# Attention in a four-stage kernel: the maxima lead by 10 tiles in place of 12, and half of the row transfers are issued by ScalarE

## The chip, the cores and the metric

The kernel runs on one core of one Trainium2 chip. The metric is the device time of one execution in microseconds (us): the median of several executions. A core has five engines that run their own instruction streams and meet only at semaphores: TensorE (PE; PEld is its weight load), VectorE (DVE), ScalarE (ACT), GpSimd (POOL) and the sync engine (SP), which computes nothing and issues transfers. An instruction that issues a transfer (a DMA) stands in the stream of the engine that issues it; the transfer itself runs on 16 DMA engines.

## The reference

The reference is a transformer of four stages on `x` of 4 x 1024 x 256: attention, a ternary feed-forward layer, a state-space layer, and a mixture of 16 experts. The change is in the attention alone:

```python
q = (x @ Wq).reshape(Bx, Tx, H, d).transpose(0, 2, 1, 3)     # H = 16 heads, d = 16
k = ...; v = ...
attn = (jnp.einsum('bhqc,bhkc->bhqk', q1, k_eff1) + jnp.einsum('bhqc,bhkc->bhqk', q2, k_eff2)) * scale
attn = jax.nn.softmax(attn, axis=-1)
out = jnp.einsum('bhqk,bhkd->bhqd', attn, v)
```

## The kernel before

The attention works in 16 **units**, each of four heads of one batch. A unit is computed twice over.

The **first pass** (`first_pass`, L2184) computes scores with queries on the partitions, in 32 **tiles** per unit, each of one head and 128 queries against all 1024 keys: two matmuls of 512 columns. VectorE reduces each tile to the negated maximum of every row (L2035). Two tiles fit in PSUM (`PAIRS = 2`), so a tile waits for the reduction of the tile two before it. A group of 16 tiles (`AHEAD`) covers half a unit, that is one half of the queries (`qc`) of four heads. When a group is complete, GpSimd splits the maxima into a high and a low part (`negated_rows`, L2100), VectorE turns them by a transpose (`turn_rows`, L2042, two tiles after the group's last, `TURN = 2`), and the rows are copied by DMA (L2137) from `nmT` to rows 48 and 49 of each half of the query buffer `KQ`: eight transfers (`ROWS`), each 2 x 8 x 32 elements, four for each half `y` of the partitions.

The **second pass** (L2238) computes the scores transposed, in 64 **blocks** per unit, each 128 keys against 512 queries of one head. The copied rows are part of its operand, so that the maximum is subtracted inside the matmul. ScalarE takes the exponential of a block (L2073) into `PR`, and TensorE weighs the values with it (L2220, in two parts for each step of four blocks). Three blocks fit in PSUM (`SLOTS = 3`): block `s` waits for the exponential of block `s - 3`. Twice per half unit ScalarE copies a half of the sums out (`keep_heads`, L2060), behind the exponentials of blocks 0 and 2.

One loop on TensorE weaves the two: block `s`, then one matmul of the tile that lies `AHEAD + LEAD` tiles on, then in every second block a part of the weighing. So two blocks go with one tile, and `LEAD` says how many tiles a group's maxima are done before the group's own scores begin. Ahead of the loop TensorE computes tiles 2 to `AHEAD + LEAD - 1` alone; at the end of the loop, where no tile is left, it repeats tiles of the last unit (`again`), so the loop is equally long for any `LEAD`. The order on each engine is the order in which the code is written.

The sync engine does, for each unit: eight transfers of heads done (`heads`, L2148 and L2149), nine loads of a later unit (L229), the rows of `(u, 1)`, nine loads, the rows of `(u + 1, 0)`. The group's first block waits for all eight rows:

```python
if kt == 0 and h == 0:
    pe.wait_ge(row_loaded[u % RING], 16 * ROWS * (QC * (u // RING) + qc + 1))
if BLOCKS * u + s >= SLOTS:
    pe.wait_ge(exp_done, BLOCKS * u + s - SLOTS + 1)
```

Of the kernel before, what the change touches and what calls it, by code (L numbers as in the profile page):

```python
# [6 lines left out]
F32 = mybir.dt.float32  # L7
# [9 lines left out]
P = 128  # L17
# [14 lines left out]
UNITS = BATCH * H // HG  # L32
# [3 lines left out]
QC = SEQ // BANK  # L36
PARTS = 2
PAIR_Q = [0, 1, 0]
PAIR_K = [0, 0, 1]
KROWS = len(PAIR_Q) * HD  # L40
AROWS = KROWS + PARTS
HALF = P // 2
HR = HG // 2
RING = 3
# [95 lines left out]
def transformer_kernel(nc, ins, out):  # L140
# [27 lines left out]
    with outer:  # L168
# [10 lines left out]
        with mid:  # L179
            ffw = FeedForwardWeights(sbuf, mid)  # L180
            with ExitStack() as st:
# [80 lines left out]
                with ExitStack() as s2:  # L262
# [6 lines left out]
                    def banks_free(eng, n):  # L269
                        if n < 3 * DK:  # L270
                            eng.wait_ge(lo_ready, 2 * DK * NC + n)
                        else:
                            eng.wait_ge(v_kept, NC + 1)
                    att = attention(nc, sem, s2, sbuf, ps, KQ, queries, kq_loaded, load_qk, V, slot, sums, maxima, packed, heads_moved, weighed,
                                    invert_sums, spread_inverses, weigh_heads, ffw, ident, projected, parts_stored, banks_free)
                    def opening_sync(sp):
# [1714 lines left out]
def attention(nc, sem, stack, sbuf, ps, KQ, queries, kq_loaded, load_qk, V, slot, sums, maxima, packed, heads_moved, weighed, invert_sums, spread_inverses, weigh_heads, ffw, ident, projected, parts_stored, banks_free):  # L1991
# [10 lines left out]
    mx, nmp, nmT = maxima.mx, maxima.nmp, maxima.nmT  # L2002
# [3 lines left out]
    vo_set, ones_ready = sem("vo_set"), sem("ones_ready")  # L2006
    row_loaded = [sem(f"row_loaded{r}") for r in range(RING)]
    st_done, exp_done, pv_done = sem("st_done"), sem("exp_done"), sem("pv_done")
    max_done, red_done = sem("max_done"), sem("red_done")
    nm_hi, nm_lo, nm_turned = sem("nm_hi"), sem("nm_lo"), sem("nm_turned")  # L2010
# [6 lines left out]
    LOADS = (2 + 2 * QC) * len(PAIR_Q)  # L2017
    QH = QT // QC
    AHEAD = HG * QH
    LEAD = 12  # L2020
    TURN = 2
    WPARTS = 2
    PART = BANK // WPARTS
# [2 lines left out]
    st_bank = lambda u, s: ST_BANK + (BLOCKS * u + s) % SLOTS  # L2026
    half = lambda h, n: slice(HALF * (h // HR), HALF * (h // HR) + n)
    of_tile = lambda kq, h, q: kq[half(h, KROWS), q // QH, h % HR, q % QH * P:(q % QH + 1) * P]

    def vector(dve):  # L2030
        def reduce(u, t):
            h, q = order[t]
            b = max_bank(u, t)
            dve.wait_ge(max_done, MAXES * u + t + 1)
            nc.vector.tensor_reduce(mx[:, u % RING, h * QT + q:h * QT + q + 1], ps[:, b:b + 2].rearrange("p a n -> p (a n)"), AX, ALU.max, negate=True).then_inc(red_done, 1)  # L2035

        def turn_rows(u, qc):

            dve.wait_ge(nm_lo, QC * u + qc + 1)
            if u > 0:  # L2040
                dve.wait_ge(row_loaded[(u - 1) % RING], 16 * ROWS * (QC * ((u - 1) // RING) + qc + 1))
            nc.vector.transpose(nmT[:, qc], nmp[:, qc].rearrange("p y a m -> p (y a m)")).then_inc(nm_turned, 1)  # L2042

        for u in range(UNITS):
            for t in range(MAXES):
                reduce(u, t)
                if u % 2 == 1 and u > 1 and t == 2 * LEAD:
                    invert_sums(dve, u // 2 - 1)
                groups, past = divmod(MAXES * u + t + 1, AHEAD)
                if groups > 0 and past == TURN:  # L2050
                    turn_rows((groups - 1) // QC, (groups - 1) % QC)
        turn_rows(UNITS - 1, QC - 1)

    def scalar(act):
        def keep_heads(u, qc, part):

            act.wait_ge(pv_done, WPARTS * (STEPS * u + KT * (qc + 1) - 1) + part + 1)
            if u > 0:
                act.wait_ge(heads_moved, 16 * MOVES * u)
            nc.scalar.copy(OT[:, qc * BANK + part * PART:qc * BANK + (part + 1) * PART],  # L2060
                           ps[:, OT_BANK, part * PART:(part + 1) * PART]).then_inc(ot_kept, 1)

        ffw.magnitudes(nc, act, kept)
        for h in range(2):
            parts_stored(act, h)
        for u in range(UNITS):
            for s in range(BLOCKS):
                step, h = s // HG, s % HG
                kt = step % KT
                act.wait_ge(st_done, BLOCKS * u + s + 1)  # L2070
                if h == 0 and STEPS * u + step >= 2:
                    act.wait_ge(pv_done, WPARTS * (STEPS * u + step - 1))
                nc.scalar.activation(PR[:, kt % 2, h], ps[:, st_bank(u, s)], ACT.Exp).then_inc(exp_done, 1)  # L2073
                if kt == 0 and h % 2 == 0:
                    if step > 0:
                        keep_heads(u, 0, h // 2)
                    elif u > 0:
                        keep_heads(u - 1, 1, h // 2)
        for part in range(WPARTS):
            keep_heads(UNITS - 1, 1, part)  # L2080
# [46 lines left out]
                pool.wait_ge(weighed, PIECES * ((u - 1) // 2))  # L2127

    def sync(sp):
        def rows(u, qc):  # L2130
            sp.wait_ge(nm_turned, QC * u + qc + 1)
            for g in range(P // 32):
                for y in range(2):
                    row, of = HALF * y + KROWS, 32 * g + 16 * y
                    src = nmT[of:of + PARTS * HR * QH, qc]
                    dst = queries(u % RING)[row:row + PARTS, qc].rearrange("a h (q n) -> a (h q) n", n=P)[:, :, 32 * g:32 * (g + 1)]
                    sp.dma_start(dst.bitcast(F32), src).then_inc(row_loaded[u % RING], 16)  # L2137

        def heads(u):


            sp.wait_ge(ot_kept, WPARTS * QC * (u + 1))
            b, g = u // UPB, u % UPB
            pair = u // 2
            for h in range(HG):
                to = HALF * (g % 2) + HD * h
                one = 2 * HD * h + HD
                sp.dma_start(slot(b)[to:to + HD, g // 2], OT[2 * HD * h:2 * HD * h + HD, :]).then_inc(heads_moved, 16)  # L2148
                sp.dma_start(packed[to:to + HD, pair % 2], OT[one:one + 1, :].rearrange("a (r n) -> a r n", r=HD)).then_inc(heads_moved, 16)  # L2149

        projected(sp)
        ffw.load(sp)
        for h in range(2):
            parts_stored(sp, h)
        rows(0, 0)
        for u in range(UNITS):
            if u == 0:
                sp.wait_ge(ones_ready, 2)
            if u > 0:
                heads(u - 1)  # L2160
            for some in (range(LOADS // 2), range(LOADS // 2, LOADS)):
                if u + 2 < UNITS:
                    sp.wait_ge(st_done, BLOCKS * u)
                    load_qk(sp, u + 2, (u + 2) % RING, some)
                if some.start == 0:
                    rows(u, 1)
            if u + 1 < UNITS:
                rows(u + 1, 0)
            if u == 2:
                sp.wait_ge(ffw.steps, ffw.quantised)  # L2170
            if u > 0 and u % 2 == 0:
                spread_inverses(sp, u // 2 - 1)
        heads(UNITS - 1)
# [21 lines left out]
    def tensor(pe):  # L2195
# [27 lines left out]

        for t in range(PAIRS, AHEAD + LEAD):
            for k in range(QC):
# [3 lines left out]
        for u in range(UNITS):  # L2229
            kq = KQ[u % RING]  # L2230
            for s in range(BLOCKS):
# [8 lines left out]
                t, k = divmod(s, QC)  # L2240
                ahead = MAXES * u + AHEAD + t + LEAD
                if ahead < MAXES * UNITS:
# [9 lines left out]
    def heads_kept(pe):  # L2252
        pe.wait_ge(ot_kept, WPARTS * QC * UNITS)

    return AttentionPrograms(vector, scalar, gpsimd, sync, tensor, first_maximum, heads_kept)


# [24 lines left out]
```

## Time and profile before

| | us |
|---|---|
| runs | 1662.2, 1668.51, 1669.74 |
| median | 1668.51 |
| the profiled execution's own time | 1661.44 |
| its span (first to last instruction) | 1659.7 |
| the attention's loop, first to last exponential | 126.2 to about 778 |
| mean granted clock of TensorE | 0.931 |

The trace gives for each instruction its start and duration. A line number is that of the kernel before; ACTq and SPq are instructions that the engine's sequencer carries out itself, such as the issue of a transfer or a wait for a semaphore.

### The profile page before, as it was taken

To read this page: it belongs to the slowest core of one execution; us is meant where nothing else is said; L and a number is where in the kernel's file an instruction comes from. 1 tells how busy PE (TensorE), PEld (TensorE's weight loads), DVE (VectorE), ACT (ScalarE), POOL (GpSimd) and SP (SyncE) were. 2 spreads that over 40 slices of the span, in tenths; PEclk is the share of its full clock that TensorE was granted. 3 is DMA by queue.
4 is the path that set the end of the run, shared out by engine and by line. 5 is a ranking of instruction groups with operands and counts; after the bars stand their busy time and mean duration, and the time that the engine had idled before them with its cause. 6 is when DMAs were issued, how large, how long until landed. Compare 5 with 4: busy or idle time off the path is not lost. (4 is left out here: it accounts for less than half of the span.)

```text
span 1659.7 us, 39722 instructions
## 1 busy us (share of the span) xinstructions
PE 1495.5 (90%) x14095; PEld 986.6 (59%) x14097; DVE 1160.0 (70%) x2105; ACT 988.0 (60%) x2035; POOL 428.2 (26%) x703
## 2 busy tenths in 40 slices
PE   6999999999999999999999968899695499999990
PEld 5843333333333333334788867888584399999980
DVE  7687999999999999980888857454486622222225
ACT  3426888888888888886355613344232355555543
POOL 3144501010101010100112234333330155555540
PEclk9967999999999999999999976899896599999995
DMA  6951223232322323210200002343457222222218
GB/s 222 280 173 26 47 47 61 47 60 48 60 52 55 61 49 62 48 23 9 27 1 0 1 15 53 105 105 96 124 193 234 89 70 70 70 70 70 73 57 306
DMA packets 117063, 135.27 MB, mean 81 GB/s; under 512 B 29540, under 2 KB 85880, under 8 KB 116792
## 3 DMA queue, kind: packets, MB, share of 16 engines
q1 hardware_dynamic: 104152, 107.60, 25.3%
q0 software_dynamic: 7584, 20.72, 3.9%
q10 hardware_dynamic: 5184, 4.98, 0.9%
q8 instruction: 96, 1.57, 0.4%
q14 instruction: 47, 0.39, 0.1%
HBM read 92.23 MB, written 36.04 MB: 77 GB/s over the span
## 5 line engine op out<-in xcount | busy, mean ns | idle before, releaser
L2035 DVE TENSOR_REDUCE mx<-ps 128x1 f32<-128x1024 f32 x512 | 622.8, 1221 | 26.5 <-PE ps L2184 21.2
L2073 ACT ACTIVATE PR<-ps 128x512 f32<-128x512 f32 x1024 | 557.1, 599 | 89.1 <-PE ps L2238 34.1
L2184 PE MATMUL ps<-KQ 48*128 48x512 f32 x1024 | 390.5, 463 | 3.4 <-DVE mx L2035 3.0
L2238 PE MATMUL ps<-KQ 50*128 50x512 f32 x1024 | 380.4, 451 | 0.2 <-DMA KQ<-nmT 0.2
L2220 PE MATMUL ps<-PR,VO 128*32 128x256 f32 x4096 | 331.1, 395 | 9.2 <-ACT PR L2073 8.7
L2238 PEld LDWEIGHTS ps<-KQ 50*128 50x128 f32 x1024 | 155.5, 187 | 218.0 <-ACT PR L2073 200.4
L2220 PEld LDWEIGHTS ps<-PR,VO 128*32 128x32 f32 x4096 | 80.9, 108 | 196.6 <-ACT PR L2073 98.7
L2184 PEld LDWEIGHTS ps<-KQ 48*128 48x128 f32 x1024 | 159.4, 192 | 21.2 <-DVE mx L2035 20.5
L1927 PEld LDWEIGHTS ps<-e_xinT,e_w 128*128 128x128 f32 x1264 | 155.0, 193 | 5.7 <-issue 1.7
L1927 PE MATMUL ps<-e_xinT,e_w 128*128 128x128 f32 x1264 | 155.7, 277 | 1.1 <-ACT e_xinT L1841 1.1
L1917 PE MATMUL ps<-eW,e_hiddenT 128*128 x632 | 149.4, 380 | 0.6 <-DVE e_hiddenT L1893 0.6
L2100 POOL CAST nmp<-mx 128x16 fp32r<-128x16 f32 x32 | 6.3, 196 | 530.2 <-DVE mx L2035 406.3
L1893 DVE TENSOR_SCALAR e_hiddenT<-ps,b1T 128x128 f32<-128x128 f32 x158 | 48.1, 346 | 105.4 <-PE ps L1927 99.3
L1917 PEld LDWEIGHTS ps<-eW,e_hiddenT 128*128 128x128 f32 x632 | 114.0, 190 | 13.1 <-issue 0.8
L1886 DVE TENSOR_TENSOR e_y<-ps,b2b 128x256 f32<-128x256 f32 x79 | 33.6, 425 | 115.0 <-PE ps L1917 114.7
L1823 POOL DMA_INDIRECT expert_outputs<-e_y,y_row x79 | 78.0, 987 | 123.6 <-DVE e_y L1886 123.2
L1333 PE MATMUL ps<-W 64*64 64x72 f32 (+7 forms) x1024 | 87.2, 259 | 12.0 <-DVE W L1143 8.3
L1818 POOL DMA_INDIRECT e_xin<-expert_inputs,token x79 | 76.9, 973 | 79.5 <-POOLq L1814 53.5
L1849 ACT COPY e_w<-eW 128x1024 f32 x79 | 82.6, 1046 | 22.4 <-issue 16.4
L1335 PE MATMUL ps<-W 64*64 64x64 f32 (+7 forms) x1152 | 90.9, 252 | 2.5 <-issue 2.5
L1841 ACT COPY e_xinT<-ps 128x256 f32<-128x256 f32 x79 | 29.4, 372 | 85.0 <-PE ps L1908 85.0
L1335 PEld LDWEIGHTS ps<-W 64*64 64x64 f32 x1152 | 70.9, 154 | 7.0 <-issue 7.0
(290 smaller groups left out, 2103.6 us busy)
## 6 DMA issues: line engine op xcount, KB each, us to landing
qk_parts<-parts SPq DMA_DIRECT2D x8, 2048.0 KB, 8.5
TB<-toeplitz_lines SPq DMA_DIRECT2D x32, 512.0 KB, 6.3
KQ<-qk_parts SPq DMA_DIRECT2D x96, 128.0 KB, 4.6
KQ<-qk_parts SPq DMA_DIRECT2D x192, 64.0 KB, 2.4
eW<-in_L_ffn_W SPq DMA_DIRECT2D x16, 512.0 KB, 10.5
eW<-in_L_ffn_W SPq DMA_DIRECT2D x8, 1024.0 KB, 11.9
e_got<-expert_outputs SPq DMA_DIRECT2D x16, 512.0 KB, 8.2
X<-in_L_attn_x SPq DMA_DIRECT2D x8, 512.0 KB, 4.3
```

What stands on the lines that cost most here:

```text
L1333: nc.tensor.matmul(pair(0, h)[r, s % HS, 0:c + BLK], W2[r, s, P:P + BLK], W1[r, s, P - c:P + BLK], start=True, stop=True, skip_group_check ...
L1335: last = nc.tensor.matmul(pair(1, h)[r, s % HS, 0:c + BLK], W1[r, s, P:P + BLK], W2[r, s, P - c:P + BLK], start=True, stop=True, skip_grou ...
L1818: nc.gpsimd.indirect_dma_start(xin[:, r], None, xrows, bass.IndirectOffsetOnAxis(ap=token[:, k:k + 1].bitcast(U32), axis=0)).then_inc(x_lo ...
L1823: nc.gpsimd.indirect_dma_start(y_rows, bass.IndirectOffsetOnAxis(ap=y_row[:, k:k + 1].bitcast(U32), axis=0), y[:, z], None).then_inc(store ...
L1849: nc.scalar.copy(w1[:, z].rearrange("p k h -> p (k h)"), W1[:, ds(e, 1)].rearrange("p a k h -> p (a k h)")).then_inc(w1_kept, 1)
L1917: last = nc.tensor.matmul(ps[:, Y_BANK[z], 0:D], hT[:, z, j], W2[:, ds(e, 1), j, :].rearrange("p a d -> p (a d)"), start=(j == 0), stop=(j ...
L1927: last = nc.tensor.matmul(ps[:, bank, j % HK * P:(j % HK + 1) * P], w1[:, z, dk, j * P:(j + 1) * P], xT[:, z, dk], start=(dk == 0), stop=( ...
L2035: nc.vector.tensor_reduce(mx[:, u % RING, h * QT + q:h * QT + q + 1], ps[:, b:b + 2].rearrange("p a n -> p (a n)"), AX, ALU.max, negate=Tr ...
L2073: nc.scalar.activation(PR[:, kt % 2, h], ps[:, st_bank(u, s)], ACT.Exp).then_inc(exp_done, 1)
L2184: made = nc.tensor.matmul(ps[:, max_bank(u, t) + k], of_tile(queries(u % RING), h, q), kq[half(h, KROWS), 0, h % HR, k * BANK:(k + 1) * BA ...
L2220: last = nc.tensor.matmul(ps[2 * HD * h:2 * HD * (h + 1), OT_BANK, cols], VO[:, u % 2, kt, h], PR[:, kt % 2, h, cols], start=(kt == 0 and ...
L2238: nc.tensor.matmul(ps[:, st_bank(u, s)], kq[half(h, AROWS), 0, h % HR, kt * P:(kt + 1) * P], queries(u % RING)[half(h, AROWS), qc, h % HR] ...
```

## The change

`LEAD` falls from 12 to 10. The function `rows` moves out of `sync`, takes the engine and the half `y`, and issues four transfers per call. The sync engine calls it for `y = 0` at the places where it issued all eight; ScalarE calls it for `y = 1`, once ahead of its loop and then ahead of the exponential of block 20 (rows of `(u, 1)`) and of block 52 (rows of `(u + 1, 0)`) of each unit.

```diff
-    LEAD = 12
+    LEAD = 10
...
+    def rows(eng, u, qc, y):
+        eng.wait_ge(nm_turned, QC * u + qc + 1)
+        for g in range(P // 32):
+            row, of = HALF * y + KROWS, 32 * g + 16 * y
+            src = nmT[of:of + PARTS * HR * QH, qc]
+            dst = queries(u % RING)[row:row + PARTS, qc].rearrange("a h (q n) -> a (h q) n", n=P)[:, :, 32 * g:32 * (g + 1)]
+            eng.dma_start(dst.bitcast(F32), src).then_inc(row_loaded[u % RING], 16)
...
+        act.wait_ge(ones_ready, 2)
+        rows(act, 0, 0, 1)
         for u in range(UNITS):
             for s in range(BLOCKS):
                 step, h = s // HG, s % HG
+                for qc in range(QC):
+                    if s == QC * (AHEAD * (2 - qc) + TURN - LEAD) + 4 and u + 1 - qc < UNITS:
+                        rows(act, u + 1 - qc, qc, 1)
                 kt = step % KT
                 act.wait_ge(st_done, BLOCKS * u + s + 1)
...
-        rows(0, 0)
+        rows(sp, 0, 0, 0)
...
                 if some.start == 0:
-                    rows(u, 1)
+                    rows(sp, u, 1, 0)
             if u + 1 < UNITS:
-                rows(u + 1, 0)
+                rows(sp, u + 1, 0, 0)
```

ScalarE's stream in the middle of a half unit, before. A row is a line of the code with its operation, the tile that it writes and what it waits for; `x3` is three in a row:

```order
L2073 ACTIVATE PR<-ps 128x512 [waits pv_done,st_done]
L2073 ACTIVATE PR<-ps 128x512 [waits st_done] x3
L2073 ACTIVATE PR<-ps 128x512 [waits pv_done,st_done]
L2073 ACTIVATE PR<-ps 128x512 [waits st_done] x3
L2073 ACTIVATE PR<-ps 128x512 [waits pv_done,st_done]
```

The same place after the change; L2086 is the exponential's new line number and L2036 the issue of a row:

```order
L2086 ACTIVATE PR<-ps 128x512 [waits pv_done,st_done]
L2086 ACTIVATE PR<-ps 128x512 [waits st_done] x3
L2036 DMA KQ<-nmT 2x8x32 [waits nm_turned]
L2036 DMA KQ<-nmT 2x8x32 x3
L2086 ACTIVATE PR<-ps 128x512 [waits pv_done,st_done]
```

Four issues have come between the exponential of block 19 (or 51) and that of block 20 (or 52): 31 times in the loop, and once ahead of it.

TensorE's stream where the loop begins, before (L447 is a projection of the stage in front; the first row with L2238 is the first block of the loop):

```order
L2184 MATMUL ps<-KQ 128x512 x2
L447 MATMUL ps<-wfT,xT 128x256 x12
L2184 MATMUL ps<-KQ 128x512 x52
L2238 MATMUL ps<-KQ 128x512
L2184 MATMUL ps<-KQ 128x512
```

And after:

```order
L2188 MATMUL ps<-KQ 128x512 x2
L447 MATMUL ps<-wfT,xT 128x256 x12
L2188 MATMUL ps<-KQ 128x512 x48
L2242 MATMUL ps<-KQ 128x512
L2188 MATMUL ps<-KQ 128x512
```

The stretch of first-pass matmuls ahead of the loop is four matmuls, two tiles, shorter.

## Rows read from the trace of the kernel before

**Rows 1.** The page's costliest groups: DVE's reductions (busy us, mean ns).

```profile
L2035 DVE TENSOR_REDUCE mx<-ps 128x1 f32<-128x1024 f32 x512 | 622.8, 1221 | 26.5 <-PE ps L2184 21.2
```

**Rows 2.** Two windows: busy us (instructions) of PE, PEld, DVE, ACT, POOL; clock.

```profile
720.00:740.00 20.00, 19.73 (x194) 7.33 (x192) 19.52 (x19) 17.71 (x35) 0.42 (x2) 1.00 0.08 19
740.00:760.00 20.00, 19.73 (x194) 7.24 (x194) 3.28 (x4) 17.71 (x35) 3.75 (x10) 1.00 0.14 27
```

**Rows 3.** Timeline, PE in the loop (start us, us): two blocks and the next.

```profile
301.43 0.49 PE L2238 MATMUL ps<-KQ 50*128 50x512 f32 x1
...
301.76 0.39 PE L2238 MATMUL ps<-KQ 50*128 50x512 f32 x1
...
302.09 0.64 PE L2220 MATMUL ps<-PR,VO 128*32 128x256 f32 x8
302.66 0.49 PE L2238 MATMUL ps<-KQ 50*128 50x512 f32 x1
```

**Rows 4.** Timeline, ACT and DVE from the start of a half unit.

```profile
296.21 0.37 ACT L2060 COPY OT<-ps 128x256 f32<-128x256 f32 x1 [0.24 <-PE ps L2220]
296.48 1.09 ACT L2073 ACTIVATE PR<-ps 128x512 f32<-128x512 f32 x2
...
297.71 1.61 ACT L2073 ACTIVATE PR<-ps 128x512 f32<-128x512 f32 x3
299.50 12.89 ACT L2073 ACTIVATE PR<-ps 128x512 f32<-128x512 f32 x21 [0.18 <-PE ps L2238]
303.37 0.20 DVE L2042 STREAM_TRANSPOSE nmT<-nmp 128x32 f32<-128x32 f32 x1
```

**Rows 5.** Timeline, narrow windows of ACT: exponentials of two blocks, then the next.

```profile
301.96 1.08 ACT L2073 ACTIVATE PR<-ps 128x512 f32<-128x512 f32 x2
303.19 0.60 ACT L2073 ACTIVATE PR<-ps 128x512 f32<-128x512 f32 x1
```

**Rows 6.** The row transfers' issues on SP: all, and one run of eight.

```profile
L2137 SPq DMA_DIRECT2D KQ<-nmT x256: 596/611/839, 114.4 to 750.5; - x128
187.10 5.29 SPq L2137 DMA_DIRECT2D KQ<-nmT  x8
```

**Rows 7.** Issues by ACT in the last stage (ns min/median/max), two with neighbours.

```profile
L1963 ACTq DMA_DIRECT2D out<-X x8: 378/422/1342, 1632.9 to 1654.6; - x8
1632.86 0.32 SPq L1957 DMA_DIRECT2D e_got<-expert_outputs  x1
1632.87 0.43 ACTq L1963 DMA_DIRECT2D out<-X  x1
1650.11 1.71 ACT L1970 ACTIVATE e_second<-e_got,weight 128x256 f32<-128x256 f32 x4 [1.69 <-DMA e_got<-expert_outputs]
1651.37 0.38 ACTq L1963 DMA_DIRECT2D out<-X  x1
```

**Rows 8.** A wait of ScalarE for `heads_moved` (L2059), and the exponentials beside it.

```profile
L2059 ACTq EVENT_SEMAPHORE  x1: 17/17/17, 296.6 to 296.6; - x1
L2073 ACT ACTIVATE PR<-ps x2: 603/604/605, 296.5 to 297.0; 128x512 f32<-128x512 f32 x2
```

**Rows 9.** Timeline, the end of the stretch ahead of the loop.

```profile
114.29 12.62 DVE L2035 TENSOR_REDUCE mx<-ps 128x1 f32<-128x1024 f32 x10
125.45 0.62 PE L2238 MATMUL ps<-KQ 50*128 50x512 f32 x1
```

**Rows 10.** Windows by clock: two in the loop, two in later stages; columns as rows 2.

```profile
130.00:140.00 10.00, 10.00 (x56) 3.30 (x52) 5.69 (x6) 4.52 (x9) 6.36 (x9) 0.50 0.01 3
150.00:155.00 5.00, 5.00 (x52) 1.82 (x48) 4.98 (x5) 4.33 (x8) 0.00 (x0) 1.00 0.00 0
824.00:832.00 8.00, 5.70 (x18) 4.36 (x19) 7.56 (x14) 4.77 (x8) 0.00 (x0) 0.79 0.00 0
964.00:968.00 4.00, 3.04 (x25) 3.04 (x26) 0.91 (x1) 0.00 (x0) 2.82 (x4) 1.00 0.00 0
```

**Rows 11.** Who waited for the row transfers (us, times).

```profile
  PEld ps L2238: 2.3, 5
```

More of the change, by code:

```diff
@@ L2129, in sync @@
     def sync(sp):
[L2130 to L2137, printed above, removed]
         def heads(u):
```

## The prediction

> **What bounds the kernel now.** I read first which engine paces the attention's loop, then where a wait that the change moves would land. In the windows of the loop TensorE is busy 19.73 of 20 us at full clock, VectorE 19.52 and ScalarE 17.71 [rows 2]. VectorE looks like a second bound: a reduction takes 1.221 us [rows 1], and two blocks pass each 1.23 us (PE's block matmul starts at 301.43 and 302.66) [rows 3]. The second window of rows 2 tells them apart: in it VectorE has next to nothing to do, 3.28 us, and TensorE still does 194 matmuls in 20 us, as before. So TensorE paces the loop by itself, and time that it loses there comes back nowhere: afterwards it can go no faster than 1.23 us per two blocks.
>
> ScalarE has 11% of slack on the mean, but what counts is how late one exponential may be. Take as zero the start of a block pair on TensorE. Its second block starts at +0.33 and lasts 0.39, so it is done at +0.72 [rows 3]. The two exponentials start at +0.53 (301.96) and at +1.02 (a pair of 1.08 us whose second lasts about 0.59, so it starts at 302.45); the next pair's first starts at +1.76 (303.19) and ends 0.60 later [rows 3, 5].
>
> **The two tiles less ahead of the loop.** There VectorE paces: ten reductions in 12.62 us, 1.26 us a tile [rows 9]. Two fewer take 2.5 us off the start of the loop (125.45). The early part of the loop runs at the low clock, 1.2 GHz: 56 matmuls in 10 us against 97 at full clock, and full clock is there by 150 us [rows 2, 10]. If the rise comes 2.5 us earlier too, all of 2.5 us is won; if it stays where it is, work is won at the rate 56/97, 1.4 us. I take 2.0.
>
> **The sync engine's half.** Its issues stand 5.29 us for eight, (5.29 - 0.61)/7 = 0.67 us from one to the next [rows 6]; four less at each place free 2.7 us on its queue. That buys only what now waits for the rows: 2.3 us over the whole kernel at the weight load [rows 11], of which most is hidden behind matmuls under way. I take 0.5, between 0 and 2.3. The lead that is two tiles (2.5 us) shorter costs nothing on this side, since the issues end 2.7 us earlier. In the sync engine's queue the loads behind the rows move earlier too, and nothing waits for them.
>
> **ScalarE's half, which decides.** When does ScalarE's first issue start? The rows are turned, before, at 303.57; blocks 6 to 26 of that half unit start from 299.50 and each takes (12.89 - 0.60)/20 = 0.615 us, so that is (303.57 - 299.50)/0.615 = 6.6 blocks on, within block 12 [rows 4]. (The three groups of exponentials in front are blocks 0, 1 to 2 and 3 to 5.) With `LEAD` at 10 it is four blocks later, within block 16: ahead of the issues, which stand behind the exponential of block 19. So `nm_turned` is no wait. How far may the sequencer run ahead of the engine? It passes instructions still being executed: one transfer was issued at 1651.37 while a run of four activations lasted from 1650.11 to 1651.82 [rows 7]. But it does not pass one whose own wait is open: the wait for `heads_moved` stands behind the exponential of block 2, asks for something long done, and is carried out at 296.6, when block 2's scores have just come and its exponential (297.0) still stands behind that of block 1 [rows 8]. So the first issue comes when block 19's scores are done, at +0.8 of the pair 18 and 19.
>
> How long are four issues? ScalarE issues none of this shape in the trace. The nearest rows: the same transfers from the sync engine, 0.61 us (0.596 to 0.839) [rows 6], and ScalarE's own of another shape, 0.378 to 0.43, once 1.342 [rows 7]. I take the same transfer's: the shape decides more than the engine, as the first runs of both engines are alike (0.32 to 0.43 in rows 7). Four take 3 x 0.67 + 0.61 = 2.62 us, to +3.42. The exponential of block 20 starts about 0.1 later, +3.52, in place of +1.76: 1.76 late. It ends at +4.12. Block 23 waits for it (three slots); its turn would be at 2 x 1.23 + 0.33 = +2.79. With 0.05 for the semaphore it starts at +4.17, and **TensorE stands still for 1.4 us**. Behind it the tile's second matmul and so VectorE's reduction wait too, as does the weighing. ScalarE then does its exponentials 0.49 apart and is level again before the next wait.
>
> The issues stand at 31 places in the loop. At block 20 of unit 0 the clock is low and two blocks, which are 12 matmuls, take 10 / 56 x 12 = 2.1 us [rows 10]: block 23's turn is at +4.9, and the exponential, even a us later than above, is not missed; 30 places are left: 30 x 1.4 = 42 us. Bounds: at 0.42 us an issue (0.38 and a gap) four end at +2.5, and block 23 is 0.4 to 0.5 late, some 13 us in all; at 0.84 and a gap each, +4.3, 2.3 us late, 69 us. A bound at nothing is the second rival.
>
> Do the two queues disturb each other? At 1632.86 both issued within 10 ns, and ScalarE's took 0.43, against 0.378 alone [rows 7]: 0.05 an issue, 0.2 a place, 6 us in all, within the bounds. The Trainium skill (Perfetto Trace Analysis, DMA Instruction, HWDGE) has the sequencers share one descriptor generator under a lock, and would make each of two issues at once wait for the other. The trace agrees in sign, but with a tenth of such a wait.
>
> **The sum.** 42 - 2.0 - 0.5 = +39.5 us on the profiled execution's 1661.44: 1701. The median of the runs shown lies 7.1 above that execution, so the changed kernel's median should lie between 1701 and 1708; I say **1705**. A measurement of this kernel tells about 0.5%, 8 us, from no change.
>
> **Rivals.** *The issues are hidden* (0.16). If ScalarE's sequencer ran on past open waits, the issues would begin when the rows are turned, 0.6 into block 16, which is at -0.33; they would end at +2.3, block 20's exponential would start at +2.4 and end at +3.0, and TensorE would stand for 0.25 us: 7.5 us in all, 1661.4 + 7.5 - 2.5 = 1666, or 1670 for the median, no change. For it speaks that the issues were given four blocks to spare; against it the wait of rows 8. The Trainium skill (TensorE: Matmul & The Clock Gate, Architectural detail) gives ScalarE a queue of 8 instructions, which would hold the exponentials up to block 19 with ease and gives this rival's time if issues may pass what waits in it; rows 7 show a queue, rows 8 that what follows does not pass an open wait.
>
> *The clock falls too* (0.08). In a later stage the clock fell where TensorE stood idle for 2.3 us: mean 0.79 over 8 us, so 3.4 us at 1.2 GHz; where it stood for 0.96 us it kept 2.4 GHz [rows 10]. A stop of 1.4 us lies between. If each of 30 stops cost 3.4 us at the low clock, 3.4 x (1 - 56/97) = 1.4 us more each, it is +82: 1743 to 1750.
>
> *Faster* (0.06). This needs the issues at no cost, at most 0.35 us each: four would end at +0.8 + 1.4 = +2.2 and block 20's exponential, at +2.3 to +2.9, would just not hold block 23. Then 2.5 us ahead of the loop and up to 2.3 of waits are won; and if the clock rose as soon as the loop begins, 22 us at the low rate would shrink by 22 x (1 - 56/97) = 9 us. Together 5 to 14 us, 1648 to 1656. From 0.35 an issue on it decides; every row is above that but one of the sync engine (0.32).
>
> **How the numbers follow.** The forecast has 0.70, with 1680 to 1735 as its own range (bounds 13 and 69). The range over all goes down to the hidden case and leaves out the faster one and most of the clock's: 1668 to 1735. Slower by over 0.5% (over 1677): 0.70 less a little for its lower end, and 0.08, 0.75. Within 0.5%: 0.20. Faster: 0.05.
>
> **What would show it.** Right: in the profile after, ScalarE's four issues stand about 0.65 us apart, the first about 0.8 us after the block pair starts; behind them comes the exponential 1.8 us late, and TensorE's idle time before L2242 or before its weight load grows by about 1.4 us at each of 30 places, released by ScalarE; the loop's windows show about 93% of the matmuls per us; the loop starts 2.5 us earlier. Wrong: issues of under 0.4 us, or issues that begin before block 19's scores are done, or a granted clock under 1.00 between 150 and 780 us.

## The result, and the profile after

The changed kernel takes 1773.61 us in the median of four runs (1755.11 to 1812.54), against 1668.92 us before: a ratio of 1.056 (interval 1.051 to 1.060). That ratio is over the two lower runs of the changed kernel alone, 1755.11 and 1761.71; the other two, 1785.51 and 1812.54, had a lower mean clock still (0.882 and 0.868, against 0.897 and 0.901), and the ratios below leave out such executions likewise, while each median counts all. The profiled execution took 1761.71 us, span 1760.0 us, 100.3 us longer than before. The forecast was 1705, in 1668 to 1735: the sign was right and the size far too small.

The place that the prediction worked out, in the timeline (start, duration, engine, what). TensorE's rows L2242 are blocks 18 to 23; ACTq L2036 are ScalarE's issues:

```profile
279.79 0.49 PE L2242 MATMUL ps<-KQ 50*128 50x512 f32 x1
...
280.12 0.39 PE L2242 MATMUL ps<-KQ 50*128 50x512 f32 x1
...
280.56 0.62 ACTq L2036 DMA_DIRECT2D KQ<-nmT  x1
280.81 0.59 ACT L2086 ACTIVATE PR<-ps 128x512 f32<-128x512 f32 x1
281.02 0.49 PE L2242 MATMUL ps<-KQ 50*128 50x512 f32 x1
...
281.22 1.92 ACTq L2036 DMA_DIRECT2D KQ<-nmT  x3
281.35 0.39 PE L2242 MATMUL ps<-KQ 50*128 50x512 f32 x1
...
282.25 0.50 PE L2242 MATMUL ps<-KQ 50*128 50x512 f32 x1
...
283.24 2.77 ACT L2086 ACTIVATE PR<-ps 128x512 f32<-128x512 f32 x5 [1.84 <-PE ps L2242]
283.89 0.49 PE L2242 MATMUL ps<-KQ 50*128 50x512 f32 x1 [1.14 <-ACT PR L2086]
```

With 279.79 as zero: the first issue comes at +0.77 (forecast +0.8), while block 19's exponential has not begun; the fourth ends at 283.14, +3.35 (+3.42); block 20's exponential starts at +3.45 (+3.52), and block 23, due at 282.58, starts at 283.89, 1.31 us late (1.4). These rows show the chain step by step. The last row names ScalarE as the releaser, and PE's idle time as 1.14 us, because block 22's matmul is still counted as busy.

Over the loop, the same view of waits as [rows 11] was taken from, 160 to 850 us (engine, line, who for, us in total, times, longest):

```profile
PE ps L2242 <- ACT PR L2086: 31.2, 26, 1.4
```

And the windows of the loop, columns as in [rows 2], with one ahead of them and one stop close up:

```profile
95.00:150.00 55.00, 50.30 (x244) 20.66 (x244) 49.22 (x44) 25.55 (x57) 29.97 (x51) 0.69 0.37 91
...
200.00:300.00 100.00, 95.66 (x780) 33.70 (x778) 79.86 (x71) 71.79 (x139) 15.21 (x51) 0.83 0.23 44
300.00:400.00 100.00, 95.44 (x750) 33.54 (x746) 76.68 (x68) 69.03 (x133) 7.46 (x30) 0.80 0.25 45
400.00:500.00 100.00, 94.24 (x830) 33.99 (x830) 85.71 (x76) 75.60 (x145) 8.29 (x34) 0.91 0.25 45
500.00:600.00 100.00, 93.10 (x834) 33.69 (x838) 84.97 (x74) 77.50 (x149) 7.86 (x32) 0.93 0.25 44
600.00:700.00 100.00, 95.67 (x780) 33.81 (x777) 79.90 (x71) 71.75 (x139) 7.91 (x32) 0.83 0.24 45
700.00:800.00 100.00, 92.95 (x890) 34.33 (x886) 91.44 (x81) 81.50 (x158) 9.69 (x42) 1.00 0.25 48
800.00:850.00 50.00, 47.45 (x384) 16.76 (x384) 33.74 (x30) 35.44 (x69) 4.16 (x12) 0.83 0.09 19
...
204.00:207.00 3.00, 1.80 (x18) 0.69 (x20) 1.52 (x3) 1.30 (x3) 2.46 (x10) 1.00 0.03 4
207.00:215.00 8.00, 8.00 (x52) 2.62 (x48) 4.82 (x4) 4.46 (x9) 1.00 (x3) 0.53 0.01 2
215.00:236.00 21.00, 21.00 (x120) 6.88 (x120) 12.37 (x11) 10.96 (x22) 1.83 (x10) 0.50 0.41 61
...
306.00:348.00 42.00, 42.00 (x242) 13.81 (x240) 24.61 (x21) 22.11 (x42) 1.83 (x10) 0.51 0.26 45
...
500.00:507.00 7.00, 6.12 (x46) 2.00 (x46) 4.05 (x4) 4.88 (x10) 0.00 (x0) 0.76 0.01 2
```

The window from 700 to 800 is what had been forecast: clock 1.00 and 890 matmuls in 100 us, 93% of the 956 before (4778 in 500 us over the same loop). All the other windows from 200 us on hold fewer per us, and a lower clock. The clock fell right behind a stop: TensorE does 1.80 us of work between 204 and 207, then runs at 0.53, and stays at 0.50 through 21 us in which it is never idle. Of the 650 us between 200 and 850, (0.17 + 0.20 + 0.09 + 0.07 + 0.17) x 2 x 100 + 0.17 x 2 x 50 = 157 us went at 1.2 GHz; before, none of the loop's 500 us from 200 to 700 did.

Not every stop did this. In windows of 1 us the clock is low in eight stretches between 160 and 850 us, and each begins within 2 us behind the end of a stop; the other 18 of the 26 stops left it at 1.00. The eight stretches differ much: 3.4 us at 1.2 GHz for the shortest (the window from 500 to 507), 41 us for the longest (306 to 348), 157 in all. The stops themselves are alike, 1.13 to 1.40 us of idle time.

These parts nearly add up to the change. Stops: the 26 of the line above and one more at 850.44, at about 1.4 us, 38. Low clock: at 56 matmuls per 10 us in place of 97 [rows 2, 10], 157 x (1 - 56/97) = 66 us. Against them the front: by 150 us TensorE had done 244 matmuls since 95 us, against 188 before, worth 56 / 9.7 = 5.8 us, because the loop began 2.2 us earlier (123.26) and the clock rose earlier. 38 + 66 - 6 = 98 us, of the 100.3 measured.

### The profile page after: what moved, and what is told of

Its sections match the earlier page's. It is cut to its first block and busy times, and to the rows that moved or that the text cites. A ratio compares the mean times of both kernels' runs of the same rounds, so it can differ in the third digit from the quotient of the medians.

```text
span 1760.0 us, 39715 instructions
## 1 busy us (share of the span) xinstructions
PE 1559.4 (89%) x14091; PEld 1003.3 (57%) x14093; DVE 1162.6 (66%) x2105; ACT 985.5 (56%) x2035; POOL 428.3 (24%) x703
## 5 line engine op out<-in xcount | busy, mean ns | idle before, releaser
L2086 ACT ACTIVATE PR<-ps 128x512 f32<-128x512 f32 x1024 | 554.1, 600 | 182.3 <-PE ps L2242 143.9
L2242 PE MATMUL ps<-KQ 50*128 50x512 f32 x1024 | 420.2, 488 | 33.6 <-ACT PR L2086 33.5
L2188 PE MATMUL ps<-KQ 48*128 48x512 f32 x1024 | 428.2, 499 | 3.8 <-DVE mx L2043 3.8
L2224 PE MATMUL ps<-PR,VO 128*32 128x256 f32 x4096 | 360.9, 427 | 7.7 <-ACT PR L2086 7.3
L2242 PEld LDWEIGHTS ps<-KQ 50*128 50x128 f32 x1024 | 170.7, 203 | 286.2 <-ACT PR L2086 253.1
L2188 PEld LDWEIGHTS ps<-KQ 48*128 48x128 f32 x1024 | 174.1, 208 | 19.7 <-DVE mx L2043 19.0
L1333 PEld LDWEIGHTS ps<-W 64*64 64x64 f32 x1024 | 65.6, 149 | 24.6 <-DVE W L1143 12.9
```

What stands on the lines that cost most here:

```text
L1333: nc.tensor.matmul(pair(0, h)[r, s % HS, 0:c + BLK], W2[r, s, P:P + BLK], W1[r, s, P - c:P + BLK], start=True, stop=True, skip_group_check ...
L2188: made = nc.tensor.matmul(ps[:, max_bank(u, t) + k], of_tile(queries(u % RING), h, q), kq[half(h, KROWS), 0, h % HR, k * BANK:(k + 1) * BA ...
L2224: last = nc.tensor.matmul(ps[2 * HD * h:2 * HD * (h + 1), OT_BANK, cols], VO[:, u % 2, kt, h], PR[:, kt % 2, h, cols], start=(kt == 0 and ...
L2242: nc.tensor.matmul(ps[:, st_bank(u, s)], kq[half(h, AROWS), 0, h % HR, kt * P:(kt + 1) * P], queries(u % RING)[half(h, AROWS), qc, h % HR] ...
```

## The experiments

Theory: ScalarE's four issues in a row outlast the slack of the next exponential, TensorE stops for 1.3 to 1.4 us, and the stop costs the clock. Rivals: the shorter lead makes the rows late; each issue costs its time wherever it stands; the clock falls for another reason. The ratios are to the kernel before on the same chip, which had medians of 1663.27 (the first four experiments), 1667.67 (two issues at a time, three and one, the first copies, LEAD 8) and 1665.37 us (the longer copies, LEAD 9).

**The lead alone.** Edit to the kernel before:

```diff
-    LEAD = 12
+    LEAD = 10
```

> The kernel before with LEAD 10 and nothing else: all eight row transfers stay with the sync engine. Theory (ScalarE's issues stop TensorE, and the stops cost the clock): no stop, clock 1.00 from about 150 us to the end of the loop, 1663 to 1671 us, that is the time of before less up to 2.5 us. Rival (the shorter lead makes the rows late): TensorE waits for KQ<-nmT at many group starts, and most of the 105 us of the change are here too, 1700 us or more.

1659.34 us, ratio 0.998 (0.994 to 1.001); that is below the range expected, but on this chip the kernel before, too, took 1663.27 us and not 1668.92. The loop is at full clock as before, and the waits for the rows at the weight load are 2.2 us, for 2.3:

```profile
200.00:700.00 500.00, 493.30 (x4775) 182.70 (x4772) 487.20 (x430) 442.98 (x846) 53.44 (x211) 1.00 0.29 54
```

The lead loses nothing. A gain of 0.15% (2.5 us) would lie inside this interval; it is not shown.

**ScalarE's half alone.** Edit to the changed kernel:

```diff
-    LEAD = 10
+    LEAD = 12
```

> The changed kernel with LEAD back at 12: ScalarE still issues four rows at a time, at blocks 16 and 48. Theory: the same stops of 1.3 to 1.4 us at 30 places and the same falls of the clock, 1745 to 1810 us. Rival (the shorter lead makes the rows late): 1669 us, or 1710 if only the stops are left.

1789.07 us, ratio 1.070 (1.063 to 1.078), mean clock 0.85 from 200 to 700 us. So the loss comes with the issues by ScalarE and not with the lead. It is no smaller than the change's: in its trace 14 of 28 stops were followed by a low clock, 188 us in all from 160 to 890, where the changed kernel has 8 and 157.

**One issue at a time.** The four issues stand ahead of blocks 20, 22, 24 and 26 (and 52 to 58):

```diff
-                    if s == QC * (AHEAD * (2 - qc) + TURN - LEAD) + 4 and u + 1 - qc < UNITS:
-                        rows(act, u + 1 - qc, qc, 1)
+                    n, rest = divmod(s - (QC * (AHEAD * (2 - qc) + TURN - LEAD) + 4), 2)
+                    if rest == 0 and 0 <= n < 4 and u + 1 - qc < UNITS:
+                        rows(act, u + 1 - qc, qc, 1, range(1 * n, min(1 * (n + 1), 4)))
```

The last argument of `rows` is new: it says which of the four transfers a call issues.

> The changed kernel, but ScalarE's four issues of a half unit stand apart, one ahead of the exponentials of blocks 20, 22, 24 and 26 (52, 54, 56, 58). Theory (what costs is that four issues in a row outlast the slack of one exponential): one issue of 0.62 us ends 1.4 us after the pair's start, before the next exponential's turn at 1.76, so no stop, clock 1.00 in the loop, 1662 to 1671 us. Rival (each issue costs its 0.62 us wherever it stands, 124 x 0.62 = 77 us, or the second queue disturbs the transfers): 1710 us or more.

1665.04 us, ratio 1.000 (0.997 to 1.003), clock 1.00 from 200 to 700 us with 4764 matmuls, against 4778. The same 124 issues, on the same engine, cost nothing that shows when each fits the slack. The rival that prices each issue at 0.62 us falls.

**The stop filled.** Five more matmuls behind the tile's matmul in blocks 22 and 54:

```diff
-                if ahead < MAXES * UNITS:
-                    first_pass(pe, ahead // MAXES, ahead % MAXES, k)
-                else:
-                    again(ahead, k)
+                for _ in range(1 + (5 if s in (22, 54) else 0)):
+                    if ahead < MAXES * UNITS:
+                        first_pass(pe, ahead // MAXES, ahead % MAXES, k)
+                    else:
+                        again(ahead, k)
```

> The changed kernel with five more matmuls after the tile's matmul in blocks 22 and 54, each a repeat of that same matmul into the same bank, so nothing else is computed: TensorE has work of 5 x 0.21 = 1.1 us in the stop of 1.3 us that follows. Theory (about 40 us are the stops themselves and the rest the clock that falls because TensorE stands idle in them): the stops' time stays, the clock stays at 1.00, 1700 to 1715 us. Rival (the clock falls for another reason, or the rest of the loss is something else): low clock as in the changed kernel, 1745 us or more.

1709.80 us, ratio 1.023 (1.018 to 1.027). The medians are further apart, 46.5 us or 2.8%. ScalarE's side is as in the changed kernel, the same issues and the same gap, but TensorE now works through it: the sixfold row is the tile's matmul with its five repeats, and block 23 starts 1.64 us behind block 22, as at 283.89 above:

```profile
277.06 0.62 ACTq L2036 DMA_DIRECT2D KQ<-nmT  x1
...
277.72 1.92 ACTq L2036 DMA_DIRECT2D KQ<-nmT  x3
279.74 7.70 ACT L2086 ACTIVATE PR<-ps 128x512 f32<-128x512 f32 x13 [1.83 <-PE ps L2242]
...
278.75 0.50 PE L2242 MATMUL ps<-KQ 50*128 50x512 f32 x1
278.75 1.66 PE L2188 MATMUL ps<-KQ 48*128 48x512 f32 x6
280.39 0.50 PE L2242 MATMUL ps<-KQ 50*128 50x512 f32 x1
```

Its loop in one window shows the clock at 1.00:

```profile
200.00:700.00 500.00, 492.42 (x4559) 191.45 (x4557) 456.73 (x401) 410.37 (x790) 50.01 (x196) 1.00 0.27 50
```

A half unit is 16 pairs of blocks of 12 matmuls in the trace, 192, and now 192 + 5. So 4559 of them are 23.1 half units of 21.6 us, against 500 / (4778 / 192) = 20.1 us before: 1.5 us a half unit. The delay by ScalarE is all there, and only TensorE's idleness is gone. The profiled executions are 1761.71 - 1709.83 = 52 us apart. Against the 66 us worked out above stand two more stops here (30 places, as the one in unit 0 fell into low clock, where the changed kernel's trace has 28), 3 us, and a slower start of this trace, 179 matmuls from 95 to 150 us for 244, 6.7 us: 66 - 3 - 6.7 = 56.

**How long a stop may be.** Two issues ahead of blocks 20 and 24 (52 and 56), then three and one, with the edit of the one-at-a-time experiment at two and at three a place, four blocks apart:

> The changed kernel, with ScalarE's four issues in two pairs, ahead of the exponentials of blocks 20 and 24 (52 and 56). Theory (the issues cost only what outlasts the slack): two issues end 0.77 + 0.65 + 0.62 = 2.04 us after the pair's start, the exponential runs from 2.14 to 2.74, and block 23's turn is at 2.80: a stop of under 0.1 us, 1663 to 1671 us, clock 1.00 in the loop. Rival (the cost goes by the number of issues): half of the changed kernel's stops at twice the places, 1700 us or more.

> The changed kernel, with three of ScalarE's issues ahead of block 20 (52) and the fourth ahead of block 24 (56). Theory: three issues end at 2.69, the exponential ends at 3.40, block 23 stands 0.65 us, at 30 places 20 us: 1683 to 1692 us if a stop of that length leaves the clock at 1.00. If it costs the clock too: 1700 us or more, with stretches of 0.50 in the loop. I expect the first.

1666.48 us, ratio 1.001 (0.998 to 1.003), for two at a time; 1681.89 us, ratio 1.009 (1.006 to 1.012), for three and one. The loop's window of two at a time, then that of three and one:

```profile
200.00:700.00 500.00, 492.33 (x4708) 183.91 (x4704) 481.76 (x424) 431.20 (x833) 55.11 (x214) 1.00 0.29 53
```

```profile
200.00:700.00 500.00, 481.19 (x4596) 177.64 (x4596) 471.45 (x414) 423.58 (x814) 54.71 (x212) 1.00 0.29 53
```

The waits of three and one for the exponentials:

```profile
PE ps L2243 <- ACT PR L2087: 15.0, 30, 0.6
```

A half unit takes 500 x 192 / 4708 = 20.4 us with two and 20.9 us with three. Two at a time thus cost 0.3 us a place, some 9 us over the loop, which the ratio does not show (a loop that begins two tiles earlier goes against it). Three cost 0.8 us a place; their time is 1 us below the range expected. Neither costs the clock.

**Stops without a transfer.** The kernel before, and on ScalarE ahead of blocks 16 and 48 (`idle` is a new buffer that nobody reads, `X2` the first columns of `X`):

```diff
+                if s in (16, 48):
+                    if 2 * u + s // 32 > 0:
+                        act.wait_ge(idled, 4 * (2 * u + s // 32))
+                    for n in range(4):
+                        nc.scalar.copy(idle[:, 344 * n:344 * (n + 1)], X2[:, 0:344]).then_inc(idled, 1)
```

> The kernel before (LEAD 12, all rows with the sync engine), and ahead of the exponentials of blocks 16 and 48 of each unit four copies of 128 x 344 elements on ScalarE into a buffer that nobody reads, about 1.9 us together. Theory (the clock falls because TensorE stands idle, whatever holds ScalarE up): stops of about 1.3 us at 31 places and falls of the clock as in the changed kernel, 1740 to 1810 us. Rival (the clock, or the rest of the loss, has to do with transfers issued by ScalarE): stops only, clock 1.00, 1700 to 1712 us.

1693.56 us, ratio 1.017 (1.012 to 1.022), clock 1.00. My expectation was wrong by the length of the copies: they follow each other in 0.38 us, 1.5 us for four, not 1.9. The stop at one place:

```profile
269.79 1.61 ACT L2076 CAST idle<-X 128x344 bf16<-128x344 f32 x4
...
270.75 0.50 PE L2246 MATMUL ps<-KQ 50*128 50x512 f32 x1
271.96 0.50 PE L2246 MATMUL ps<-KQ 50*128 50x512 f32 x1 [0.70 <-ACT PR L2081]
```

Its waits for the exponentials over the loop:

```profile
PE ps L2246 <- ACT PR L2081: 21.9, 31, 0.7
```

The pair's second matmul starts 1.21 us behind its first in place of 0.33, so it is 0.9 us late, with TensorE idle for 0.7, and 31 such places keep the clock. This left both sides open, so the copies were made longer:

```diff
-                        act.wait_ge(idled, 4 * (2 * u + s // 32))
+                        act.wait_ge(idled, 6 * (2 * u + s // 32))
...
+                    act.wait_ge(idled, 6 * (2 * u + s // 32) + 2)
+                    nc.scalar.copy(idle[:, 0:344], X2[:, 0:344]).then_inc(idled, 1)
+                    nc.scalar.copy(idle[:, 344:408], X2[:, 0:64]).then_inc(idled, 1)
```

> The kernel of the stops without transfers, whose stops came out at about 0.8 us and left the clock at 1.00, with two more copies (128 x 344 and 128 x 64) on ScalarE at each place, so that TensorE stands for about 1.3 us, as long as in the changed kernel. Theory (a stop of that length costs the clock, whatever makes it): stretches of 0.50 in the loop and 1740 us or more. Rival (it takes ScalarE's transfers): clock 1.00 and some 40 us of stops, 1705 to 1715 us.

1811.64 us, ratio 1.080 (1.075 to 1.085). The waits at the stops:

```profile
PE ps L2249 <- ACT PR L2084: 33.1, 27, 1.2
```

Two windows of its loop:

```profile
200.00:300.00 100.00, 92.80 (x888) 34.20 (x888) 90.12 (x81) 90.91 (x187) 15.70 (x54) 1.00 0.23 45
...
600.00:700.00 100.00, 95.45 (x756) 33.19 (x752) 76.36 (x68) 77.15 (x158) 7.94 (x32) 0.80 0.25 45
```

In this loop ScalarE issues no transfer, the lead is 12, and the clock falls as in the changed kernel. So stops by themselves are enough, whatever makes ScalarE late. The first window says that not every such stop does it: its stops are as long, and it kept 1.00. Over the loop ten of these 27 stops, all of 1.22 to 1.24 us of idle time, were followed by a low clock, for 3.4 to 38 us.

**Less lead still.** Two runs went after the small gain ahead of the loop. First LEAD 8 with one issue at a time (ahead of blocks 24, 26, 28 and 30):

> The kernel of one issue at a time with LEAD 8 in place of 10, the issues ahead of blocks 24, 26, 28 and 30 (56 to 62). Theory: two more tiles less ahead of the loop, 2.5 us less; the last row is issued some 3 us ahead of the group's first block and lands in about 2, so no new wait: 1658 to 1668 us. Rival (the rows come too late): TensorE waits for KQ<-nmT at most of the 32 group starts, each up to 1 us, 1670 us or more.

1723.66 us in the median of four (1691.64 to 1741.26). The rival came true, and I had miscounted: the last issue comes 1.7 us ahead of the group's first block (at the place below 590.64, with the block due at 592.33), not 3. What waited:

```profile
PE ps L2243 <- DMA KQ<-nmT: 28.1, 18, 5.3
```

The costliest place in the timeline:

```profile
590.64 0.62 ACTq L2036 DMA_DIRECT2D KQ<-nmT  x1
590.61 0.64 SPq L202 DMA_DIRECT2D sums<-softmax_inverses  x1
597.67 0.79 PE L2243 MATMUL ps<-KQ 50*128 50x512 f32 x1 [5.28 <-DMA KQ<-nmT]
```

The last row transfer was issued at 590.64, in the same moment as the spreading of the inverses (512 KB), and was waited for until 597.67. All five waits of over 4 us stand behind such a pair of issues, within 0.04 us of each other; that the large transfer holds up the small one is argued from this, not tried. The clock fell in or behind each of the five, for 3.4 to 24 us: 0.86 in the window from 600 to 700 us. Then LEAD 9, with all rows at the sync engine:

> The kernel before with LEAD 9 and all rows with the sync engine. Theory: three tiles less ahead of the loop, 3.8 us less than before, and no new wait, since the rows of (u, 1) are issued when the sync engine is free, as before, and those of (u + 1, 0) end some 5 blocks ahead: 1657 to 1667 us, ratio 0.995 to 1.000. Rival (less lead makes rows late, as with LEAD 8 and ScalarE's late issues): waits for KQ<-nmT of over 10 us in all and a ratio above 1.005.

2545.74 us, ratio 1.529 (1.525 to 1.532), with no wait for the rows: far outside the range expected, and not by the rival either. TensorE in the loop:

```profile
401.24 0.79 PE L2238 MATMUL ps<-KQ 50*128 50x512 f32 x1
401.83 0.62 PE L2184 MATMUL ps<-KQ 48*128 48x512 f32 x1
402.26 0.62 PE L2238 MATMUL ps<-KQ 50*128 50x512 f32 x1
402.69 0.62 PE L2184 MATMUL ps<-KQ 48*128 48x512 f32 x1
```

And in the windows:

```profile
400.00:500.00 100.00, 100.00 (x401) 44.89 (x404) 40.88 (x36) 40.58 (x71) 5.60 (x20) 0.50 0.11 20
```

Each matmul now starts behind the one before; with an even lead a block (L2242) and a tile (L2188) start together, as both do at 278.75 in the filled stop. The clock is not the whole of it: at the same 0.50 the changed kernel did 120 matmuls in 21 us, 571 in 100, against 401. By the code an odd lead puts the tile's head (`order` alternates between the halves `y`) into the same half of the partitions as the block's. That the halves are what lets two run side by side is argued from this, not tried by itself. So the gain of less lead stays unmeasured there. Why the clock stays at 0.50 over 100 us in which TensorE is counted as busy throughout is open too.

## Why the prediction had the stops right and the clock wrong

- **TensorE bounds the loop, and lost time comes back nowhere:** right. The stops add to the half unit in full in every experiment at full clock.
- **Two tiles less:** forecast 2.0; the loop began 2.2 us earlier. The clock also rose earlier in this trace, so that 5.8 us were won by 150 us, but the traces differ as much among themselves: from 95 to 150 us the six with LEAD 10 show 179 to 244 matmuls, the four with LEAD 12 178 to 200. With the lead alone the ratio is 0.998, not distinguishable from 1.
- **The sync engine's half:** forecast 0.5, of no account. The waits for the rows fell from 2.3 to 1.0 us at the weight load.
- **When the first issue starts:** right, +0.77 for +0.8. The sequencer did not pass the open wait of block 19, so the rival of hidden issues fell.
- **What an issue costs on ScalarE:** right: 0.62 us in the median (one of 128 took 1.52), 0.65 from one to the next, for 0.61 and 0.67. The same shape costs the same on both engines, and ScalarE's transfers of another shape in [rows 7] 0.38 to 0.43.
- **The two queues:** the 0.43 us read as a disturbance is the ordinary length of that issue, whose median is 0.422 [rows 7], so no row showed one. In the four issues beside the sync engine's, ScalarE's took 0.62 as elsewhere.
- **The stop and the sum of the stops:** 1.31 at the place shown and 1.4 to 1.5 by the half unit, for 1.4. The filled stops measured the term alone: 38 us by the ratio, 46.5 by the medians, for 42 less 2.5. Only 28 places showed it in the changed kernel: the place in unit 0 did, as the clock had risen early there, and three others did not, since at the low clock ScalarE has slack.
- **The clock:** this step failed. The sum has no term for it. The rival *The clock falls too* had a chance of 0.08, on no row that speaks against it, and priced a fall at 3.4 us of low clock at every stop, 42 us. The runs show 66 us, from eight falls of 3.4 to 41 us behind 26 stops, and where the stop is filled the clock is 1.00 throughout. The sign that was named, a clock under 1.00 between 150 and 780 us, came.

The two neighbours of [rows 10] were also misread, because their windows cut the stops short. The timeline of before has TensorE idle for 1.32 us where the clock stayed, and for 2.64 where it fell, not 0.96 and 2.3:

```profile
826.30 1.61 PE L814 MATMUL ps<-f_xT,fvT 128*80 128x512 f32 x4 [2.64 <-DVE f_xT L703]
...
964.96 4.28 PE L875 MATMUL ps<-wpT,sq 128*128 128x256 f32 x34 [1.32 <-DVE V L747]
```

The idle time of the new stop, 1.2 us, is thus shorter than one that kept the clock. Read rightly these rows would have spoken even more for the forecast, and been no better guide: one stop that kept the clock says little when 8 of 26 such stops lose it. The rows for a better price of a fall were there: in the first part of the loop [rows 10] TensorE had been busy 10.00 of 10 us and was still at 0.50, from 125 to about 147 us. In the trace after it was at 0.50 through 21.00 busy us of 21.

A smaller slip: at 0.35 us an issue the prediction has block 20's exponential end at +2.9 and calls block 23, due at +2.79, just not held. By its own numbers it would be held for 0.1 to 0.2 us, so the case *Faster* needed issues of about 0.31 us.

What stays open is which stops cost the clock. Stops alike to 0.1 us did and did not, in the same trace, and the four runs of the changed kernel lie 57 us apart, the longer ones at a lower mean clock.

## What to carry to other kernels

An engine that feeds the bounding one through a few buffers has a slack per step, not per stage: work of its sequencer, such as issuing transfers, is free only in pieces that fit between two of its instructions. Here one issue of 0.65 us was free, two cost 0.3 us a time, three 0.8 and four 1.4 to 1.5. And where TensorE bounds, a stop's price is not its length. One place that kept the clock does not settle what many new ones will do: multiply the number of new stops by a share of them that falls (here 8 of 26, 14 of 28 and 10 of 27 at 1.2 us of idle time, none of 31 at 0.7) and by the length of the low stretches in the profile. When a stop can't be shortened below that, see whether it can be split, as here over more places.

## What the runs showed of the hardware

- Stops with 0.7 us of idle time (0.9 us late) every 21 us left the granted clock at 1.00 over 500 us. Stops with 1.2 us (1.3 to 1.4 late) every 21.5 us, by transfer issues or by copies alike, let it fall at 8 of 26, 14 of 28 and 10 of 27 places. One of 1.32 us in a later stage of the kernel before left it at 1.00. With the same stop filled with repeated matmuls it stayed at 1.00.
- After a fall it stayed at 0.50 for 3.4 to 41 us; in the longest TensorE was busy 42.00 of 42 us.
- ScalarE's issue of a transfer of 2 x 8 x 32 elements takes 0.62 us, nearly the same as the sync engine's 0.61. With both issuing at once ScalarE's took no longer (0.621 and 0.622 in four issues from 280.6 to 283.1), and three of the sync engine's beside them 0.615 to 0.698.
- Two matmuls of 48 and 50 rows ran side by side with an even lead, and one behind the other with an odd one: 571 against 401 matmuls in 100 us, both at 0.50.
